# VectorE's split of the first expert's gate and up weights among the tail's tiles, and two orders changed with it

## The reference, cut to what matters

```python
x = x + xattn(ctx, layernorm(x), ...)       # a selective scan over L = 512 positions, 4 batches
h = layernorm(x)                            # T = 2048 rows of H = 512
scores = softmax(h @ gate_w.T)              # E = 16 experts
topk_w, topk_idx = top_k(scores, 2)
gu = einsum('th,ehj->etj', h, w_gate_up)    # I = 352 gate columns and 352 up columns
y  = einsum('eti,eih,te->th', silu(g) * u, w_down, combine)
y  = y + swiglu(h @ shared_gate_up) @ shared_down     # SI = 704, for all rows
x  = x + y
```

## Time and profile before

| | us |
|---|---|
| median of 3 runs | 1085.01 |
| lowest, highest | 1083.24, 1085.73 |
| the profiled execution | 1088.87 |
| its span, first to last instruction | 1087.1 |
| busy in the span: PE, DVE, POOL, ACT | 913.7, 831.9, 753.9, 515.1 |

### The profile page before, as it was taken

The page is one execution under the profiler, slowest core; times in us unless marked ns, Lnnn a source line. Parts: engine busy times, 40 slices in busy tenths (PEclk is TensorE's granted clock), DMA queues, the critical chain, the costliest instruction groups (busy, mean ns, idle before and its releaser), DMA issues.

```text
span 1087.1 us, 16598 instructions
## 1 busy us (share of the span) xinstructions
PE 913.7 (84%) x4352; PEld 671.4 (62%) x4353; DVE 831.9 (77%) x1349; ACT 515.1 (47%) x959; POOL 753.9 (69%) x482
## 2 busy tenths in 40 slices
PE   5876555778889888878998899969998999998993
PEld 2222344556556556656665555639997988897992
DVE  4788999989998899988999413869888987989000
ACT  3777634544554555455555222115554545554541
POOL 3437888988888888878994200026887888887872
PEclk9996656789999899989999989989999999999996
DMA  5469821651237322552210230036676866774432
GB/s 191 181 240 338 290 87 49 229 216 49 69 103 295 107 77 77 202 214 87 64 52 29 78 128 11 20 110 190 158 210 166 235 167 184 193 221 107 77 58 39
DMA packets 69987, 152.14 MB, mean 140 GB/s; under 512 B 7585, under 2 KB 23969, under 8 KB 64306
## 3 DMA queue, kind: packets, MB, share of 16 engines
q1 hardware_dynamic: 59410, 126.97, 33.8%
q0 software_dynamic: 10528, 24.65, 11.4%
HBM read 112.80 MB, written 38.80 MB: 139 GB/s over the span
## 4 chain that ended last, share of the span: by engine, by line
PE 51%; DVE 25%; issue 14%; ACT 4%; POOL 2%; DMA 2%; DVEq 1%; ACTq 0%; SPq 0%; POOLq 0%
PE bank L665 11%; PE bank L684 8%; PE bank L611 7%; PE bank L769 6%; PE bank L771 6%; PE bank L770 6%; DVE bank L1344 5%; DVE gs L1358 4%; DVE p_acc L1286 2%; DVE e_gu_lo L1571 2%; DVE e_gu_hi L1570 2%; DVE bank L1563 2%; ACT bank L925 1%; PE bank L758 1%; PE bank L553 1%
## 5 line engine op out<-in xcount | busy, mean ns | idle before, releaser
L1151 POOL TENSOR_TENSOR dbu<-bcs,m_w 128x2048 f32<-128x2048 f32 x64 | 295.1, 4613 | 29.0 <-DVE bank L1344 25.9
L925 ACT ACTIVATE bank<-m_dt,c_a 128x512 f32<-128x512 f32 x256 | 171.3, 685 | 235.2 <-DVE gs L1358 235.2
L1344 DVE TENSOR_TENSOR_SCAN bank<-bank,dbu 128x512 f32<-128x512 f32 x192 | 230.8, 1219 | 16.5 <-ACT bank L925 15.6
L665 PE MATMUL bank<-ws_gu,f_xnT 128*128 128x352 f32 x576 | 204.8, 499 | 31.5 <-ACT f_hT L947 29.7
L611 PE MATMUL bank<-ident,gs 128*128 128x128 f32 x768 | 141.5, 320 | 57.3 <-DVE gs L1358 50.3
L611 PEld LDWEIGHTS bank<-ident,gs 128*128 128x128 f32 x768 | 107.4, 164 | 115.6 <-DVE gs L1358 71.0
L665 PEld LDWEIGHTS bank<-ws_gu,f_xnT 128*128 128x128 f32 x576 | 112.4, 208 | 82.1 <-ACT f_hT L947 30.9
L769 PE MATMUL bank<-e_gu_hi,e_xT_hi 128*128 x376 | 130.0, 346 | 8.1 <-POOL e_xT_lo L1216 5.4
L1358 DVE TENSOR_TENSOR gs<-bank,bcs 128x512 f32<-128x512 f32 x192 | 128.3, 669 | 0.0
L771 PE MATMUL bank<-e_gu_hi,e_xT_lo 128*128 x376 | 121.9, 324 | 0.0
L770 PE MATMUL bank<-e_gu_lo,e_xT_hi 128*128 x376 | 121.8, 324 | 0.0
(11 more groups left out here) (166 smaller groups left out, 1680.9 us busy)
## 6 DMA issues: line engine op xcount, KB each, us to landing
bcs<-bc_scratch SPq DMA_DIRECT2D x32, 1024.0 KB, 9.1
e_gu<-in_wgu SPq DMA_DIRECT2D x16, 1408.0 KB
e_dn<-in_wdn SPq DMA_DIRECT2D x16, 512.0 KB
out_rows<-xt SPq DMA_DIRECT2D x18, 256.0 KB, 2.1
p_x<-in_x SPq DMA_DIRECT2D x4, 1024.0 KB, 6.8
u_scratch<-p_u SPq DMA_DIRECT2D x4, 1024.0 KB, 3.9
silu_z_scratch<-p_sz SPq DMA_DIRECT2D x4, 1024.0 KB, 5.0
dt_scratch<-p_dt SPq DMA_DIRECT2D x4, 1024.0 KB, 4.8
```

Source lines behind the costliest of these rows:

```text
L665: last = mm(dst[:, 0:I], lhs[t], ws_gu[:, t, off:off + I], start=t == 0, stop=t == KH - 1)
L925: f(HS[k % RING_H][:], m_dt[:, q % 2, :], ACT.Exp, scale=c_a[:, q, n:n + 1]).then_inc(exp_done, 1)
L1151: g.tensor_tensor(part_, Bs[:, gr * GRP:(gr + 1) * GRP, :], w, ALU.mult).then_inc(dbu_ready, 1)
L1344: v.tensor_tensor_scan(to, h, dbu[:, n, :], 0.0, ALU.mult, ALU.add).then_inc(scan_done, 1)
```

## The change

It has four parts.

1. SP: `load_gu(0, 0)` is issued right behind the load of tile 14's rows ("the third tile"), ahead of `xn_store` of tile 12. `load_dn(0)` stays behind tile 15's load.
2. DVE: the stages of `split` can be chosen. The gate stage of expert 0 stands between `hidden` and `add_shared` of tile 13, the up stage between that `add_shared` and the statistics of tile 15. Behind the tables stand now the down stage of expert 0, both `hidden`s of tile 17, gate and up stages of expert 1, `add_shared` of tile 17, and the down stage of expert 1.
3. ACT: the gates of tile 13 stand ahead of `xn` of tile 12.
4. POOL: at the end `split_hidden(46)` stands ahead of `scatter(45)`.

```diff
@@ sync @@
             xt_load((first + 2, 2), B - 1)
+            sp.wait_ge(ymm_done, B * STEPS)
+            load_gu(0, 0)
             xn_store((first, 0))
             out_store((first + 1, 1))
             sp.wait_ge(out_stored, 1 + (first + 2) * 16)
             xt_load((NT - 1, TB - 1), B - 1)
-            sp.wait_ge(ymm_done, B * STEPS)
-            load_gu(0, 0)
             load_dn(0)
@@ scalar @@
+            gate((first + 1, 1), 0)
+            gate((first + 1, 1), 1)
             xn_of(0)
-            whole((first + 1, 1))
+            hT_copy((first + 1, 1), 0)
+            hT_copy((first + 1, 1), 1)
             xnT_of(0)
@@ gpsimd @@
+            split_hidden(UNITS - 1)
             scatter(UNITS - 2)
-            split_hidden(UNITS - 1)
             scatter(UNITS - 1)
@@ vector, the tail @@
+            def split(e, ring, end, stages=(0, 1, 2)):
...
+                    if stage not in stages:
+                        continue
...
-            whole((first + 1, 1))
+            for c in range(2):
+                hidden((first + 1, 1), c)
+            split(0, 0, None, (0,))
+            add_shared((first + 1, 1))
+            split(0, 0, None, (1,))
             stats((NT - 1, TB - 1), B - 1)
             whole((first + 2, 2))
@@ vector, behind the tables @@
-            split(0, 0, None)
-            whole((NT + 1, 1))
-            split(1, 1, None)
+            split(0, 0, None, (2,))
+            for c in range(2):
+                hidden((NT + 1, 1), c)
+            split(1, 1, None, (0, 1))
+            add_shared((NT + 1, 1))
+            split(1, 1, None, (2,))
```

More of the change, by code:

```diff
@@ L1448, in _, with rounded, parts @@
             first = NT - TB
+            PIECES = 2 * KH + 3
+            def split(e, ring, end, stages=(0, 1, 2)):
+                gate, up = [[(P, t, half * I, I) for t in range(KH)] for half in range(2)]
+                dn = [(n, t, 0, H) for t, (r, n) in enumerate(IT)]
+                for stage, at, raw, hi, lo, loaded, used, done, pieces in (
+                        (0, 0, e_gu[ring], e_gu_hi, e_gu_lo, gu_loaded[ring], eu_ready, gate_split, gate),
+                        (1, KH, e_gu[ring], e_gu_hi, e_gu_lo, gu_loaded[ring], eu_ready, gu_split, up),
+                        (2, 2 * KH, e_dn, e_dn_hi, e_dn_lo, None, ey_ready, dn_split, dn)):
+                    if stage not in stages:
+                        continue
+                    def rounded(j):
+                        n, t, c, w = pieces[j]
+                        if at + j > 2:
+                            dve.wait_ge(lo_done, e * PIECES + at + j - 2)
+                        v.tensor_copy(ROUNDED[(at + j) % 3][0:n, 0:w].bitcast(F32R), raw[0:n, t, c:c + w]).then_inc(rounded_done, 1)
+                    def parts(j):
+                        n, t, c, w = pieces[j]
+                        hi_part = ROUNDED[(at + j) % 3]
+                        dve.wait_ge(rounded_done, e * PIECES + at + j + 1)
+                        v.tensor_copy(hi[0:n, ring, t, c:c + w], hi_part[0:n, 0:w].bitcast(F32R))
+                        v.tensor_tensor(lo[0:n, ring, t, c:c + w], raw[0:n, t, c:c + w], hi_part[0:n, 0:w], ALU.subtract).then_inc(lo_done, 1)
+                    if loaded is None:
+                        dve.wait_ge(dn_loaded, (e + 1) * 32)
+                    else:
+                        dve.wait_ge(loaded, (e - ring) * 8 + 16)
+                    rounded(0)
+                    if end is not None:
+                        dve.wait_ge(used, 1 + end)
+                    for j in range(len(pieces)):
+                        if j + 1 < len(pieces):
+                            rounded(j + 1)
+                        parts(j)
+                    dve.wait_ge(lo_done, e * PIECES + at + len(pieces))
+                    dve.sem_inc(done, 1)
             add_shared((first, 0))
```

34 lines of the change are left out of this document (removed).

## The result

| | before | after |
|---|---|---|
| median, us | 1085.26 | 1071.60 |
| lowest, highest | 1083.24, 1085.73 | 1068.03, 1076.29 |
| the profiled execution | 1088.87 | 1076.29 |
| its span | 1087.1 | 1074.6 |

The ratio of the times is 0.988, with an interval from 0.9839 to 0.9921: the changed kernel is 13.7 us faster (8.6 to 17.5). The same kernel measured again beside other runs of the kernel before was 10.3 and 13.2 us faster.

A forecast was written before the change was run, and what follows sets the result against it. No engine bounds it everywhere; three places do: tail-to-loop hand-over, tile 13 in the tail, and the end. 0.5 + 5.0 - 0.3 + 4.0 = 9.2 us, so the median becomes 1075.8 us, range 1073.0 to 1081.0.

The forecast's parts named there:

- loop, unit 4's turn to unit 46's: From expert 2 on, DVE's further lead is spent and both engines stand to each other as before: 0 us gained.
- Tail: ACT's gates first in tile 13: second `hidden` 0.65 us earlier, not 1.75; gain taken as 0.5 us, between 0 and 0.7.
- Early load and early split: Expert 0's weights loaded and split in the tail: load there at 622.1, cost taken 0, bounds 0 and 1 us.
- rival 5: In the tail, the early load lands 2 or more us after the `hidden`s, delaying `add_shared`: 1078 us; chance 0.05.
- Hand-over: Tail to loop: `hidden`s of tile 17 end at 716.5, PE starts step 0 earlier; gain taken as 5.0 us.
- rival 2: At the entry to the loop, the gather is late by 4 us and `add_shared` waits for PE: 1079 us; chance 0.12.
- the one in bold: Tail to loop: DVE's new place for `add_shared` ends last, by a little: 728.1 against 733.65, a gain of 5.5 us.
- Clock: Before step 0 PE may idle longer, bringing a further stretch at half rate: -1.7 to 0 us, taken as -0.3.
- Rival 3: PE enters the loop at half rate for longer, costing up to 1.7 us in step 0: 1077.6 us; chance 0.08.
- Rival 1: Late in the loop, DVE keeps its 5.9 us of lead and 5.5 us of losses go: 1070.3 us; chance 0.07.
- End: POOL's last split ahead of `scatter(45)`: the last scatter starts 4.1 or 3.1 us earlier, taken as 4.0 us.
- The base and the range: Whole program: gain taken off the median of 1085.01; range 1073.0 to 1081.0 us, including 1.2 us spread either side.

The follow-up runs named there:

- b1_after_again: The changed kernel, unaltered, measured once more: 1072.34 us, ratio 0.9906, 10.3 us faster than the kernel before.
- a4_after_no_loads: The changed kernel without the loads of the weights of experts 2 to 15: 1071.98 us, ratio 0.9883 to the kernel before.
- c1_direct_split: The changed kernel with DVE rounding weights straight into the high part for all 16 experts, 2 instructions a piece instead of 3: 1099.36 us, ratio 1.0167.

## Why the prediction was right, and where it failed

| term, us gained | forecast | from the traces |
|---|---|---|
| tail, `m_x` to tables | 0.5 | 1.6 (means of 5 and 12), 0.4 in the two profiles |
| hand-over and entry, tables to unit 4's turn | 5.0 - 0.3 | 5.3 (means of 3 and 11), 5.5 in the two profiles |
| loop, unit 4's turn to unit 46's | 0 | 0.4 (means of 2 and 8), 3.6 in the two profiles |
| end, behind unit 46's turn | 4.0 | 3.4 (means of 3 and 14), 3.0 in the two profiles |
| sum | 9.2 | 10.6, with the loop's 0.4 (from unrounded means) |

For the loop, the old one with its loads took 297.2 and 293.5 us, and the new one 292.2 to 297.3 in eight executions with a mean of 294.9. The mean of the old two is 295.3. Two old traces are few: against the 292.9 of the changed kernel's own three the loop's term would be 2.4.

No run has the early split or the early load alone. That the hand-over's gain is theirs is read from the traces: tables to unit 4's turn took 44.3 to 45.5 us in the three with the old order there, the one with only the end changed among them, and 39.3 to 40.4 in the eleven with the new.

*Tail.* The mechanism was right and undersized, and the upper bound of 0.7 was too low. `hidden` 2 came at 623.20 (forecast 623.1), `add_shared` of tile 13 at 629.53 (629.4), the up stage ended at 635.4 (635.5). What was missed is that the old wait isn't a fixed 1.75 us: it was 0.25 to 1.97, and it can take the clock with it.

*Early load and early split.* Cost 0, as forecast; rival 5 didn't come. But the slack of 1.5 us wasn't there: the load took 6.8 us and not 5.3, and landed 0.1 us ahead of its first use.

*Hand-over.* `hidden`s at 715.55 to 716.07 (716.5), DVE's eighth piece done at 726.7 (727.4), `add_shared` at 728.39 (728 to 729), first turn at 730.30 (729.9), gather late by 0.7 us (1; rival 2 had 4). The step that failed here is the one in bold: PE's down product was last, not DVE, by 1.72 us in this trace and by 0.44 in `b1_after_again`. It took 8.35 us, above my upper value of 7.26, since all of it but the end ran at 0.50 and not part of it. The sum hardly notices, because the two were within 1.7 us of each other.

*Clock.* Forecast as a loss of 0.3, it was a gain of 1.4 in the profile: the half-rate time went from two stretches to one. Before, DVE's long block put 6 us of idling ahead of the turns, and the first step fell into a second stretch. This is not a property of the change alone: `b1_after_again` has 0.80 and 0.63 in its windows from 729 to 735, and its first three steps take 17.36 us, while its down product takes 7.12. What one gets back the other loses, and the sum over both, from unit 0's turn to unit 4's, is 28.3 to 28.8 us in the three traces of this kernel. Rival 3 was thus right that the clock can fall in step 0, and wrong that this costs anything on top.
The Trainium skill (TensorE: Matmul & The Clock Gate, Part 4: PE-mode transpose), by which transposes don't hold the clock up, fits the down product behind the turns at 0.50 in the changed kernel; in `b1_after_again` the window with the same turns still shows 1.00, and in `a4_after_no_loads` and `c1_direct_split` the product behind the same turns took 5.42 us, so at the full clock. The rule alone doesn't tell when the clock falls.

*Lead.* Rival 1 did not come, though its 1070.3 lies nearer to the measured 1071.6 than the forecast: that is luck. DVE's lead is spent at expert 2 (2.25 and 9.29 us), and the losses late in the loop that it would have removed are still there: PE falls behind by 5.1, 5.4 and 6.1 us at units 35 to 39 in the three traces of the changed kernel, and by 5.5 in that of the kernel before.

*End.* Right in mechanism, 0.6 us too large: the landing of `scatter(45)` took 4.88 us where I had put the 4.35 of the one before.

*The base and the range.* This is the step of the prediction that failed. The sum took its gain off 1085.01, the median of three executions, and added "the run's own spread of 1.2 us to either side", since those three lay within 2.5 us. The kernel before, executed more often, goes from 1075.9 to 1089.9 with a mean of 1082.6 over 89 executions; beside the four later groups of runs its means are 1082.1 to 1082.8. So the base lay 2.4 us too high. The median of three such executions is itself uncertain by about 2.4 us (one standard deviation; an estimate from drawing three of them at random, again and again). The changed kernel's three medians go from 1069.6 to 1072.3. The traces show where the executions differ: the scan stage, the same in every version, ends (`m_x`) between 602.2 and 608.7, the tail behind it takes 96.1 to 99.2 us in the new order, and the loop 292.2 to 297.3.

Of the 4.2 us between the forecast of 1075.8 and the measured 1071.6, 2.4 are thus the base, and 1.7 the gain, 10.9 us over all executions where I had 9.2; the tail, undersized by about 1, is the largest part of that. The gain was 13.7, 10.3 and 13.2 us in the three comparisons, and each interval holds the 10.6 of the table; so does 10.9 give or take 1.6. With twice the base's 2.4 us taken off the earliest sum, 1074.7, the range would have had to begin near 1070.

## What to carry to other kernels

When an engine is busy with work that another waits for behind it, look for work of the same engine that has no input from the critical stage, and give it a place in an earlier stage where it idles; its lead afterwards is worth only what the next engine on the path can use. An order in which a short producer stands behind work that waits for a transfer costs little in one trace and several us in another, since the wait hangs on a landing and the clock can fall behind it: judge it by several executions. Before a range is set for a difference of 1%, the spread of the unchanged kernel must be known from more than three runs.

## What the runs showed of the hardware that I had not expected

- The same cast of 128x352 from SBUF to SBUF took 330 ns beside an idle POOL and 879 ns in the mean beside a busy one, 2.34 us where it met POOL's subtraction of 1.85 us; through PSUM each of the three instructions took 510 to 522 ns beside the same POOL.
- The last three scatters of the program landed 4.3 to 4.9 us after their start; in the loop it was up to 9.7 us with the loads of the experts' weights, and at most 5.3 without them. The gather beside `load_dn(1)` was late by only 0.7 us.
- A wait of 1.97 us for ACT in the middle of 32 matmuls was followed by a granted clock of 0.71, waits of 0.25, 1.48 and 1.75 us by 1.00.
